# Attention stages of a decoder: when the load queue waits, how a batch's finishing is spread, and which engines' programs are loops

## The reference

```python
scores = jnp.einsum('bhqd,bhkd->bhqk', q, k) / jnp.sqrt(hd)
attn = jax.nn.softmax(scores, axis=-1)
out = jnp.einsum('bhqk,bhkd->bhqd', attn, v)
```

## Time and profile before

| | |
|---|---|
| time of three runs | 4847.12, 4855.64 (median), 4861.48 us |
| the profiled execution's own time, and its span | 4844.51 us, 4842.7 us |
| busy share of the span | PE 86%, DVE 59%, ACT 48%, POOL 28% |
| granted TensorE clock, mean | 0.909 of full |
| DMA packets, bytes | 332041, 486.56 MB |
| exponentials of `pyr_coarse` | 143.4 to 312.4 us |
| of `pyr_core` | 344.6 to 537.1 us |
| of `l1x_core` | 1519.6 to 1888.2 us |
| of `l2a_core` | 2325.1 to 2509.6 us |
| of `lc` | 2755.5 to 3673.6 us |
| of `l3a_core` | 3972.7 to 4142.9 us |
| of `l3x_core` | 4270.0 to 4736.8 us |

### The profile page before, as it was taken

How to read it: one execution, slowest core, us unless ns; L and a number is a source line. 1 busy time by engine, 2 the same in 40 slices (tenths; PEclk the granted TensorE clock), 3 DMA queues, 4 the chain that set the end, 5 groups by cost and what they waited for, 6 DMA issues and landing times. The chain is left out here.

```text
span 4842.7 us, 69706 instructions
## 1 busy us (share of the span) xinstructions
PE 4152.1 (86%) x20384; PEld 1973.3 (41%) x20384; DVE 2875.1 (59%) x6517; ACT 2348.2 (48%) x4572; POOL 1359.4 (28%) x1202
## 2 busy tenths in 40 slices
PE   8679866689788997797998999999998888489986
PEld 6322355377453233484233333333335554222224
DVE  4458573501667885203863378787873256388876
ACT  4337331243234775243664455454552236379993
POOL 0121141212101111101220188787883212101112
PEclk9669987799888999798898999999999899789998
DMA  8545212354133332574335521111110134523421
GB/s 289 116 99 125 63 39 35 115 203 154 45 110 85 66 67 64 202 257 152 82 77 199 183 77 62 62 62 62 62 59 1 45 107 103 142 63 94 101 52 38
DMA packets 332041, 486.56 MB, mean 100 GB/s; under 512 B 84516, under 2 KB 232596, under 8 KB 317252
## 3 DMA queue, kind: packets, MB, share of 16 engines
q1 hardware_dynamic: 321552, 443.63, 32.1%
q0 software_dynamic: 6384, 32.61, 2.1%
q10 hardware_dynamic: 3804, 6.74, 0.4%
HBM read 327.63 MB, written 143.92 MB: 97 GB/s over the span
## 5 line engine op out<-in xcount | busy, mean ns | idle before, releaser
L1406 POOL TENSOR_TENSOR lc_totals<-lc_totals,lc_weights 128x1024 f32<-128x1024 f32 (+1 forms) x320 | 623.0, 1947 | 164.1 <-DVE lc_totals L1355 133.7
L1336 DVE TENSOR_REDUCE lc_part_max<-ps 128x2 f32<-128x1024 f32 x384 | 466.3, 1214 | 218.3 <-PE ps L1181 215.9
L1315 ACT ACTIVATE lc_weights<-ps 128x1024 f32<-128x1024 f32 x384 | 393.1, 1024 | 415.9 <-PE ps L1201 402.7
L1201 PE MATMUL ps<-lc_q,lc_k 64*128 64x512 f32 x1536 | 395.3, 593 | 4.3 <-issue 4.3
L1211 PE MATMUL ps<-lc_weights,lc_v 128*64 128x512 f32 x1536 | 371.7, 605 | 0.0
L876 DVE TENSOR_REDUCE l1x_core_part_max<-ps 128x1 f32<-128x512 f32 x512 | 318.6, 683 | 59.2 <-PE ps L697 58.2
L872 DVE CUSTOM_DVE_ANT_0 l3x_core_unused<-ps,l3x_core_mask_q 128x512 f32<-128x512 f32 x512 | 331.9, 686 | 9.8 <-DVE l3x_core_row_max L880 5.9
L835 ACT ACTIVATE l3x_core_weights<-ps 128x512 f32<-128x512 f32 x512 | 329.0, 698 | 9.9 <-PE ps L764 5.9
L835 ACT ACTIVATE l1x_core_weights<-ps 128x512 f32<-128x512 f32 x512 | 266.2, 603 | 87.1 <-PE ps L764 87.1
L818 ACT ACTIVATE ps<-l3x_core_mask_k 128x512 f32<-128x512 f32 x384 | 272.3, 709 | 34.9 <-DMA l3x_core_mask_k<-in_mask_k 34.9
L697 PE MATMUL ps<-l3x_core_k,l3x_core_q 96*128 96x512 bf16 x512 | 210.4, 412 | 47.8 <-DVE l3x_core_part_max L872 29.5
(11 more groups left out here) (494 smaller groups left out, 8572.7 us busy)
## 6 DMA issues: line engine op xcount, KB each, us to landing
cf_w<-in_L1f_w SPq DMA_DIRECT2D x32, 1024.0 KB, 8.0
lc_k<-latent_k SPq DMA_DIRECT2D x32, 768.0 KB
lc_v<-latent_values SPq DMA_DIRECT2D x32, 768.0 KB, 4.9
latent_k<-feed_staged SPq DMA_DIRECT2D x64, 256.0 KB
latent_values<-feed_staged SPq DMA_DIRECT2D x64, 256.0 KB
k_heads<-proj_parts SPq DMA_DIRECT2D x40, 384.0 KB, 2.6
q_heads<-proj_parts SPq DMA_DIRECT2D x32, 384.0 KB, 2.6
q_heads<-proj_parts SPq DMA_DIRECT2D x32, 256.0 KB, 3.0
```

What stands on the lines that cost most here:

```text
L1201: mm = nc.tensor.matmul(out[j], k_tile[g % RING][strip(j), i * P:(i + 1) * P], q_tile[g % RING][strip(j), :], start=False, stop=True)
L1315: nc.scalar.activation(weights[:, i % TILES, :, :], k.ps[:, B0 + (i % 2) * HEADS:B0 + (i % 2 + 1) * HEADS, 0:nq], ACT.Exp, scale=scale).th ...
L1336: nc.vector.reduce_max(own, k.ps[:, A0:A0 + HEADS, :], AX).then_inc(a_taken, 1)
L1406: nc.gpsimd.tensor_tensor(total, total, own, ALU.add).then_inc(added_by_pool, 1)
```

## The change

It does five things.

1. SP, `group`: the wait on `pv_done` before the operand loads becomes a wait on `s_ready`, the last score product (L764) of the group before; the loads come first, then the row (stages of 512 keys), then the wait on `pv_done` and the value load.
2. PE, `turn`, and DVE, `negate`: in `pyr_coarse` (`spans`) the transposition comes after the group's first score product instead of after its first four and the last value products of the group before; in `l3a_core` (causal) after the third. In the other stages it stays.
3. The finishing of batch b-1 is laid over two batches: gather in group 0, dense load in 1, inverse (DVE) and store in 2, broadcast in 3 of batch b; normalise in groups 0 and 1, dense copies in groups 2 and 3 (four each) of batch b+1. In the last batch the old pace holds (gather and dense load in 0; store and broadcast in 1; normalise in 2 and 3; eight dense copies in 3), with the steps left over from the batch before beside it.
4. SP's and POOL's programs in `attention_stage` have no loop. DVE's loop has lead 4 and 2 turns, so one back-branch, at the end of group 7.
5. PE's program in `latent_core_stage` has no loop; ACT, DVE, POOL and SP keep theirs.

In stages of 1024 keys POOL also does `split_max` before `normalise` instead of after it.

```diff
-    FRONT, TURN = NCH * EARLY // nkt, nkt - EARLY
+    FRONT = NCH * EARLY // nkt
+    turn_at = (nkt - EARLY, heads - 2) if late_row else (0, 0) if spans else (0, heads - 2) if causal else (0, heads)
+    negate_at = (turn_at[0], turn_at[1] + 1)
...
-            def return_inverses(b):
-
-                sync.wait_ge(normed, at(b + n_carried, 0, 1, SUMS))
+            def store_inverses(b):
+
                 sync.wait_ge(inverses_in, 16 * heads * (b + n_carried) + 1)
                 sync.wait_ge(inverted, b + n_carried + 1)
                 sync.dma_start(k.inverse_sums.rearrange("j g (s n) -> (j g s) n", n=H * nq // P), dense_inverse[:, :]).then_inc(inverses_out, 16)
+
+            def spread_inverses(b):
+
+                sync.wait_ge(normed, at(b + n_carried, 0, 1, SUMS))
                 sync.wait_ge(inverses_out, 16 * (b + n_carried + 1))
...
                 before = later(b, g, -1)
                 if exists(*before):
-                    sync.wait_ge(pv_done, at(*before, nkt, nkt + ahead_tiles))
-                    if exists(*later(b, g, 1)) and not kept:
-                        load_values(*later(b, g, 1))
                     if exists(*later(b, g, RING - 1)):
+                        sync.wait_ge(s_ready, at(*before, NS, NS))
                         load_group(*later(b, g, RING - 1))
                 if exists(*later(b, g, 1)) and not late_row:
                     row(*later(b, g, 1))
+                if exists(*before) and exists(*later(b, g, 1)) and not kept:
+                    sync.wait_ge(pv_done, at(*before, nkt, nkt + ahead_tiles))
+                    load_values(*later(b, g, 1))
...
-                if g == 1 and to_finish(b - 1):
-                    return_inverses(b - 1)
-                if g == 3 and to_finish(b - 1):
-                    make_dense(b - 1)
+                if g == (0 if last(b) else 1) and to_finish(b - 1):
+                    load_dense_sums(b - 1)
+                if g == (1 if last(b) else 2) and to_finish(b - 1):
+                    store_inverses(b - 1)
+                if g == (1 if last(b) else 3) and to_finish(b - 1):
+                    spread_inverses(b - 1)
+                if g >= 2 and to_finish(b - 2):
+                    make_dense(b - 2, slice(HG * (g - 2), HG * (g - 1)))
+                if g == groups - 1 and last(b):
+                    make_dense(b - 1, slice(0, 2 * HG))
...
                 if exists(*later(b, g, 1)) and late_row and not new_mask:
                     row(*later(b, g, 1))

-            for_groups(sync, group, lead=groups, turns=B - 2)
+            for_groups(sync, group, turns=0)
...
-                    if i == 0 and g == 1 and to_finish(b - 1):
+                    if (g, i) == ((1, 0) if last(b) else (2, 1)) and to_finish(b - 1):
                         invert_dense(b - 1)

-            for_groups(dve, group, lead=2)
+            for_groups(dve, group, lead=groups, turns=B - 2)
...
-                if g >= 2 and to_finish(b - 1):
+                if late_row and exists(*later(b, g, 1)):
+                    split_max(*later(b, g, 1))
+                if g < 2 and to_finish(b - 2):
+                    normalise(b - 2, 2 * g)
+                    normalise(b - 2, 2 * g + 1)
+                if g >= 2 and last(b):
                     normalise(b - 1, 2 * g - 4)
                     normalise(b - 1, 2 * g - 3)
-                if late_row and exists(*later(b, g, 1)):
-                    split_max(*later(b, g, 1))
-
-            for_groups(pool, group, lead=groups, turns=B - 2)
+
+            for_groups(pool, group, turns=0)
...
-            for_groups(pe, group)
+            for_groups(pe, group, turns=0)
```

More of the change, by code:

```diff
@@ L499, in to_finish, with last @@
             return small and (exists(b, 0) or (carried is not None and isinstance(b, int) and b == -1))
+        def last(b):
+            return isinstance(b, int) and b == B - 1
         def first(b, g, n=1):
@@ L532, in for_groups @@
                 body(0, g)
-            with engine.Fori(0, turns) as b:
-                for g in range(lead, groups + lead):
-                    body(b + g // groups, g % groups)
+            if turns:
+                with engine.Fori(0, turns) as b:
+                    for g in range(lead, groups + lead):
+                        body(b + g // groups, g % groups)
             for n in range(lead + turns * groups, B * groups):
@@ L618, in gather_sums, with load_dense_sums @@
                 sync.dma_start(k.sums_of_weights, sums_of(b)[HD::QUAD, :, :]).then_inc(sums_out, 16)
+            def load_dense_sums(b):
                 sync.wait_ge(sums_out, 16 * (b + n_carried + 1))
                 sync.dma_start(dense[:, :], k.sums_of_weights.rearrange("j g (s n) -> (j g s) n", n=H * nq // P)).then_inc(dense_in, 16)
[L622 to L624 removed]
+            def store_inverses(b):
                 sync.wait_ge(inverses_in, 16 * heads * (b + n_carried) + 1)
@@ L630, in return_inverses, with make_dense @@
                     sync.dma_start(inverse[strip * j:strip * (j + 1), :, :], k.inverse_sums[j, :, :].partition_broadcast(strip)).then_inc(inverses_in, 16)
-            def make_dense(b):
+            def make_dense(b, some):
                 sync.wait_ge(normed, at(b + n_carried, groups, 1, SUMS))
@@ L637, in make_dense @@
                     pairs = dense_rows(carried[1], carried[0], slice((B - 1) * nq, B * nq))
-                for destination, source in pairs:
+                for destination, source in pairs[some]:
                     sync.dma_start(destination, source).then_inc(made_dense, 16)
@@ L673, in group @@
                     row(*later(b, g, 1))
-            for_groups(sync, group, lead=groups, turns=B - 2)
+            for_groups(sync, group, turns=0)
             if small and finish:
                 gather_sums(B - 1)
-                return_inverses(B - 1)
-                make_dense(B - 1)
+                load_dense_sums(B - 1)
+                store_inverses(B - 1)
+                spread_inverses(B - 1)
+                make_dense(B - 1, slice(0, 2 * HG))
             if small:
@@ L774, in group @@
                                 pass_a(*later(b, g, ahead), [n])
-                        if late_row and (i, j) == (TURN, heads - 2) and exists(*later(b, g, 1)):
+                        if (i, j) == turn_at and exists(*later(b, g, 1)):
                             turn(*later(b, g, 1))
@@ L780, in group @@
                         weigh(*later(b, g, -1), nkt - 1)
-                    if not late_row and i == 0 and exists(*later(b, g, 1)):
+                    if (i, heads) == turn_at and exists(*later(b, g, 1)):
                         turn(*later(b, g, 1))
@@ L927, in group @@
                         after = step_after(b, g, i * heads + j)
-                        if late_row and (i, j) == (TURN, heads - 1) and exists(*later(b, g, 1)):
+                        if (i, j) == negate_at and exists(*later(b, g, 1)):
                             negate(*later(b, g, 1))
@@ L936, in group @@
                             invert(*before, inverse_at.index((i, j)))
-                    if not late_row and i == 0 and exists(*later(b, g, 1)):
+                    if (i, heads + 1) == negate_at and exists(*later(b, g, 1)):
                         negate(*later(b, g, 1))
-                    if i == 0 and g == 1 and to_finish(b - 1):
+                    if (g, i) == ((1, 0) if last(b) else (2, 1)) and to_finish(b - 1):
                         invert_dense(b - 1)
-            for_groups(dve, group, lead=2)
+            for_groups(dve, group, lead=groups, turns=B - 2)
             if small:
@@ L1101, in before, with for_groups @@
             return number(b, g) is not None and number(b, g) < n
-        def for_groups(engine, body):
-            lead, turns = 2, B - 1
+        def for_groups(engine, body, turns=B - 1):
+            lead = 2
             for g in range(lead):
                 body(0, g)
-            with engine.Fori(0, turns) as b:
-                for g in range(lead, GROUPS + lead):
-                    body(b + g // GROUPS, g % GROUPS)
+            if turns:
+                with engine.Fori(0, turns) as b:
+                    for g in range(lead, GROUPS + lead):
+                        body(b + g // GROUPS, g % GROUPS)
             for n in range(lead + turns * GROUPS, B * GROUPS):
```

## The result

Four runs of the changed kernel took 4800.99 to 4812.27 us, median **4803.4**; four of the kernel before (the three above and one more) took 4847.12 to 4861.48, median 4854.9. The medians differ by 51.5 us. The ratio put on record is 0.9905, 95% interval 0.9891 to 0.9920, so 46 us less with an interval of 39 to 53, where I had forecast 66. 4803.4 lies in the range and is 13 us above the forecast of 4790. The span of the profiled execution fell from 4842.7 to 4799.2 us.

| | before | after | change | forecast |
|---|---|---|---|---|
| `pyr_coarse` | 169.0 | 132.2 | -36.8 | -42 |
| `pyr_core` | 192.5 | 185.9 | -6.6 | -5 |
| `l1x_core` | 368.6 | 377.0 | +8.4 | +5.5 |
| `l2a_core` | 184.5 | 184.9 | +0.4 | -1 |
| `lc` | 918.1 | 904.2 | -13.9 | -17 |

The account below looks back on a forecast made before the run. PE was taken to wait for the row, held up by SP's list, in `pyr_coarse`, and at back-branches in `lc`. Terms -42 - 5 - 1 - 11 - 17 + 10 = -66 us, from 4855.6 to 4790 us; range 4764 to 4818.

Parts of the forecast that it names:

- the row in `pyr_coarse`: `pyr_coarse`: PE waits 46.9 us for the row, late by SP's list; issuing it earlier gives -42 us.
- the clean groups of 11.7 and 10.3 us: `pyr_core` and `l3a_core`: the edits remove at most what good groups don't have, -5 and -11 us.
- PE's back-branches in `lc`: `lc`: straight PE code removes the stops at two back-branches, -17 us, bounds -8 and -18.
- the new wait: `l1x_core`, `l3x_core`, last batch: group 14's row stands behind a broadcast waiting for normalise; +5.5 and +4.5 us.
- Groups 12 and 13: 15: `pyr_coarse`: groups 12 and 13 together take 15 us, against 20.9 before.
- The transfers rival: `pyr_coarse`: DMA transfers bound the stage, leaving 25 of the 42 us gain, total 4807 us; chance 0.16.
- SP's and POOL's straight programs: Attention stages: removing SP's and POOL's loops is worth 0, since no wait behind their branches is seen.
- some slower clock: `l1x_core`: PE's slower clock after the 4.8 us wait at group 14, included in +5.5 us.
- DVE's and ACT's branches: one gained, one exposed: 0: `l3x_core`: DVE's two branches become one hidden by ACT's no longer, at group 8; 0 us, bounds -3 and +3.
- The rival that the other engines' branches come out from behind PE's: `lc`: two edges of 4 to 5 us remain, 8 of the 17 us lost, total 4798 us; chance 0.10.
- The slower case: `lc`: straight code starves PE, up to 144 us over 24 groups, total 4934 us; chance 0.03.

Follow-up runs that it names:

- the two repairs: Two runs on the change, 1024-key stages: SP's row of group 14 ahead of the broadcast, 4793.1 us; or POOL's normalise ahead of split_max again, 4790.7 us.
- the row's move: The change, with SP issuing the row of group 14 ahead of the broadcast in stages of 1024 keys: 4793.1 us, ratio 0.9888.
- POOL's order: The change, with POOL doing normalise ahead of split_max again in stages of 1024 keys: 4790.7 us, ratio 0.9879.

## Why the prediction was right, and where its terms were off

The direction and most of the size came from the mechanisms named: the row in `pyr_coarse`, the clean groups of 11.7 and 10.3 us as the goal of `pyr_core` and `l3a` (-6.6 and -11.3, forecast -5 and -11), PE's back-branches in `lc`, and a new wait at group 14. By the ratio the gain falls 20 us short, by the medians 14, by the stages 19. The shortfall has four sources: `pyr_coarse` (5 us), the new wait, DVE's branch in `l3x` (11 us in `l1x` and `l3x` together) and `lc` (3). The straight programs of SP and POOL were mispriced as well, the other way.

*`pyr_coarse`, -37 instead of -42.* The term that was mis-sized is "Groups 12 and 13: 15": I gave them two undisturbed groups, though the broadcast and the four dense copies that end group 11's list stand ahead of the loads of group 12 in SP's queue. They took 20.4. In the same way I charged the broadcast of batch 0 to batch 1, which took 29.5 instead of 31.5, while it made group 8, the first of batch 2, 12.0 us long. That batch 2 took 37.0 where I had 36 is in part luck, since its long groups aren't the ones that I had in the sum. The transfers rival, by which 25 us would be left, was right about group 8 and in part about group 12, and wrong about the rest of the stage, where a DMA share of 0.54 went with groups of 7.4. The runs divide the gain: undone singly, the load wait gives back 27.5, the spread finishing 9.4, the turn 6.2, which with the 9.7 of the loops is more than 36.8. That fits parts that relieve the same list; no run undoes two of the first three together.

*SP's and POOL's straight programs, 0.* "No wait behind their branches is seen" was the wrong test. With the finishing at its old pace the loops cost 13.9 us, 9.7 of them in `pyr_coarse`, and the traces place some 3 of these in the dense copies and at SP's back-branches. That SP's list is faster straight sat unseen inside my group lengths, so this stage's forecast came out partly by it and not only by the mechanism named.

*The new wait, +10.* The place and the chain were right, the size too small: 9.4 us at groups 13 and 14 of `l1x` (7.5 to 9.0 by the two repairs) and 5.6 in `l3x` by the row's move (9.5 by POOL's order, with a stage that differs by 3 us between executions). I had "some slower clock" at 0.7 us; it was 3.5. I also took POOL's order as given and saw only one of the lists that it can block.

*"DVE's and ACT's branches: one gained, one exposed: 0", bounds ±3.* With the new wait taken off, `l3x` is still 470.0 to 473.9 against 466.8 before, so this term is +3 to +7. Group 8, at DVE's branch that now stands alone, takes 32.0 us against 28.9 (30.8 to 34.0 in the other runs with the change's pace). Hiding two branches behind ACT's and exposing one was no even trade, since before the change DVE's two cost nothing of their own.

*`lc`, -14 instead of -17.* The rival that the other engines' branches come out from behind PE's was half true: it was DVE's alone, 2.2 us at each of two groups, not 4 to 5. The traces agree with the rule of the Trainium skill, "Runtime: NRT & Kernel Launch", section "Instruction fetch mechanics", that a taken branch to code outside the engine's window stalls it: PE and DVE each stopped at their own back-branches in `lc`, and straight they don't (PE's 12 us by issue are gone, in 24 groups). My reading that long bodies pay and short ones don't is too simple, though: one turn of DVE's loop in `lc` has 362 instructions in the trace and stops, one of ACT's there has 376 and shows no stop, and one of PE's in `l2a` has 662 and shows none (a stop can be hidden under a wait). The slower case, straight code that starves PE, is out.

## What to carry to other kernels

Where one queue issues loads, exchanged rows and finishing copies, list for every wait in it what stands behind, and when that is wanted: the same trap (a wait for the finishing, with urgent work of a group behind it) was sprung in three places, twice in SP's list with a row behind the wait and once in DVE's with reductions behind it, by an edit on another engine or by a better spread of the transfers. A load's slack counts from its first reader, here pass A, not from the pass for which the ring was sized. When a branch or wait is taken off one engine, look for the same one on the next engine, and move branches only to places where another's already stands.

## What the runs showed that was not expected

- Four broadcasts of 256 KB, issued within 1.8 us, land 1.3 us apart; eight loads and the row behind them land 6.6 and 6.0 us after issue instead of 3.3 and 2.3.
- Eight dense copies with register steps between them take SP 1.2 us longer in its loop than straight (6.37 against 5.18), and four loads no longer. The loops of SP and POOL together cost 13.9 us, most of which these steps don't explain.
- Straight code isn't free either. In `l3x` the groups in which DVE is straight take 29.1 to 29.2 us (groups 1 to 3, 12), those in its loop 28.9 (groups 7, 10 and 11), and with both engines straight nearly all take 29.2. The kernel before, with DVE looped from group 2 on, has 28.9 in groups 2, 3, 12 and 13. Over 13 groups that is some 4 us. What takes the 0.3 us wasn't tried. The Trainium skill, "Runtime: NRT & Kernel Launch", section "Instruction fetch mechanics", calls the fetch cost of straight code mostly hidden; whether these 0.3 us are that cost no run here shows.
- A PE wait of 5.9 us cost another 3.5 us afterwards, in 7.1 us at the lower clock.
